# A mixture of experts after an mLSTM layer: every token through every expert, or only through its two

## The reference, cut to what matters

```python
logits = xf @ Wr + br                                   # 8 experts
topk_w, topk_idx = jax.lax.top_k(logits, 2)
topk_w = jax.nn.softmax(topk_w, axis=-1)
gate = jnp.sum(jax.nn.one_hot(topk_idx, 8) * topk_w[..., None], axis=1)
h = jax.nn.relu(jnp.einsum('th,ehf->etf', xf, W1) + b1[:, None, :])   # 128 -> 256
y = jnp.einsum('etf,efh->eth', h, W2) + b2[:, None, :]                # 256 -> 128
out = jnp.einsum('te,eth->th', gate, y)
```

## Time and profile before

| | |
|---|---|
| median of the runs | 385.41 us |
| the profiled execution | 387.64 us |
| its span, first to last instruction | 385.9 us |
| mean granted TensorE clock | 0.939 of full speed |
| bytes moved by DMA | 7.10 MB, 18 GB/s over the span |
| chain that ended last | PE 61%, DVE 23%, issue 6%, ACT 3%, POOL 3% |

### The profile page before, as it was taken

The page is one execution under the profiler, slowest core; times in us unless marked ns, Lnnn a source line. Parts: engine busy times, 40 slices in busy tenths (PEclk is TensorE's granted clock), DMA queues, the critical chain, the costliest instruction groups (busy, mean ns, idle before and its releaser), DMA issues.

```text
span 385.9 us, 6042 instructions
## 1 busy us (share of the span) xinstructions
PE 343.8 (89%) x1744; PEld 275.5 (71%) x1744; DVE 281.8 (73%) x786; ACT 227.7 (59%) x412; POOL 185.6 (48%) x180
## 2 busy tenths in 40 slices
PE   2926988999899989998999989998999899887995
PEld 2814976778687858886687868786887678665783
DVE  3787457689767986689668876897668976765664
ACT  1420232777476848586567747684857685674673
POOL 7794072148543764276326833384505641573240
PEclk9975698999899998999899989998999999998998
DMA  4840000000000000000000000000000001000000
GB/s 117 268 115 2 0 1 2 0 3 0 0 3 27 0 0 0 27 0 0 0 27 0 0 0 0 27 0 0 0 27 2 0 0 31 0 0 2 27 2 27
DMA packets 8965, 7.10 MB, mean 18 GB/s; under 512 B 1195, under 2 KB 7510, under 8 KB 8950
## 3 DMA queue, kind: packets, MB, share of 16 engines
q1 hardware_dynamic: 8722, 6.78, 6.1%
q0 software_dynamic: 64, 0.07, 0.1%
q10 hardware_dynamic: 164, 0.07, 0.1%
HBM read 4.82 MB, written 2.10 MB: 18 GB/s over the span
## 4 chain that ended last, share of the span: by engine, by line
PE 61%; DVE 23%; issue 6%; ACT 3%; POOL 3%; DMA 1%; SPq 1%; DVEq 0%; POOLq 0%
PE bank L956 7%; PE bank L958 6%; PE bank L957 6%; PE bank L984 5%; PE bank L974 5%; PE bank L975 5%; PE bank L926 5%; PE bank L994 3%; DVE hg L763 3%; PE bank L911 3%; PE bank L859 2%; PE bank L933 2%; DVE hg_lo L774 2%; DVE top_d L652 2%; DVE m_row L741 2%
## 5 line engine op out<-in xcount | busy, mean ns | idle before, releaser
L424 POOL TENSOR_TENSOR hg_lo<-hg,hg_hi 128x512 fp32r<-128x512 f32 x69 | 88.8, 1289 | 89.5 <-ACT hg_hi L494 89.5
L476 ACT ACTIVATE hid<-bank,cols 128x512 f32<-128x512 f32 x128 | 87.3, 682 | 69.4 <-PE bank L958 69.2
L763 DVE TENSOR_TENSOR hg<-hid,bank 128x512 f32<-128x512 f32 x128 | 86.7, 681 | 53.0 <-PE bank L994 32.7
L494 ACT ACTIVATE hg_hi<-hg 128x512 fp32r<-128x512 f32 x128 | 79.6, 622 | 9.0 <-DVE hg L763 8.8
L956 PE MATMUL bank<-h_hi,w_hi 128*128 (+1 forms) x128 | 58.9, 460 | 0.0
L984 PE MATMUL bank<-hg_lo,w_hi 128*128 128x512 f32 x128 | 52.6, 411 | 1.0 <-DVE hg_lo L774 0.9
L974 PE MATMUL bank<-hg_hi,w_hi 128*128 128x512 f32 x128 | 52.7, 412 | 0.0
L975 PE MATMUL bank<-hg_hi,w_lo 128*128 128x512 f32 x128 | 52.0, 407 | 0.0
L957 PE MATMUL bank<-h_hi,w_lo 128*128 (+1 forms) x128 | 51.5, 403 | 0.0
L958 PE MATMUL bank<-h_lo,w_hi 128*128 (+1 forms) x128 | 51.3, 401 | 0.0
L393 POOL TENSOR_SCALAR var_eps<-mv 128x4 f32<-128x4 f32 x16 | 4.5, 278 | 87.6 <-DVE mv L555 87.6
(11 more groups left out here) (162 smaller groups left out, 626.1 us busy)
## 6 DMA issues: line engine op xcount, KB each, us to landing
out_dram<-x_all SPq DMA_DIRECT2D x8, 256.0 KB, 2.3
w_raw<-in_L_ffn_W_dram SPq DMA_DIRECT2D x1, 1024.0 KB, 9.1
x_all<-in_L_attn_x_dram SPq DMA_DIRECT2D x2, 256.0 KB, 4.2
wmod_sb<-in_L_wmod_dram SPq DMA_DIRECT2D x1, 384.0 KB, 4.9
vo_raw<-in_L_attn_Wv_dram POOLq DMA_DIRECT2D x1, 32.0 KB, 2.8
qk_raw<-in_L_attn_Wq_dram ACTq DMA_DIRECT2D x1, 32.0 KB, 2.7
vo_raw<-in_L_attn_Wo_dram POOLq DMA_DIRECT2D x1, 32.0 KB, 3.4
qk_raw<-in_L_attn_Wk_dram ACTq DMA_DIRECT2D x1, 32.0 KB, 3.1
```

The source lines that it names most:

```text
L424: g.tensor_tensor(hg_lo[k][:, :], hg[k][:, :], hg_hi[k][:, :].bitcast(fp32), ALU.subtract).then_inc(s_lo_pool, 1)
L476: a.activation(hid[n % 4][:, :], up_bank[n % 2][:, :], ACT.Relu, bias=cols[:, R_B1 + n:R_B1 + n + 1]).then_inc(s_hid, 1)
L494: a.activation(hg_hi[k][:, :], hg[k][:, :], ACT.Copy).then_inc(s_hghi, 1)
L763: v.tensor_tensor(hg[k][:, :], hid[k][:, :], gate_bank[n // NU % 2][:, :], ALU.mult).then_inc(s_hg, 1)
```

## The change

The kernel is written anew around the routing; the mathematics of the mLSTM layer is the same. Its parts:

**Ticks.** The streams follow `TICKS` = 158 steps. Row `b` starts at tick 12·b and has steps `k` = 0 to 24; so two rows are in work at once, one in its steps 12 to 23, the next in 0 to 11.

**Slots in DRAM.** At steps 20 to 22 DVE finds the two experts of each token, PE counts with a triangular matrix how many tokens went to that expert before (L1018 to L1028), and each token has a slot number for each of its experts. At steps 23 to 30 POOL issues 8 indirect DMAs for the row (L509), each scattering 128 tokens of 512 bytes into the slots of `h_slots` of the row's group.

**Groups and blocks.** Rows (0,1), (2,3), (4,5), (6,7) are groups. When a group's rows are counted, DVE makes the list of blocks (`block_list`): 23 blocks of 128 slots, each of one expert, 92 in all. SP reads the list number by number into a register (`value_load`) and issues with it, for each block, a DMA of the 128 slots (64 KB, `xl`) and one of the expert's weights (`wl`, 128 x 642 numbers, 329 KB, from `w_all` in SBUF to SBUF), and for each group 8 DMAs of zeros behind the last token of each expert. Four blocks are a quad, two blocks a pair.

**The expert layer.** For each block PE does one transpose, two matmuls of 128 columns up and two down in plain fp32, ACT two relus of 128x128. DVE copies the transposed tokens of a quad and adds the bias to its result. SP stores a quad to `y_slots`. Pairs stand two ticks apart, and one tick apart after the last row's scatter (tick 115): group 0 has ticks 47 to 69, group 1 71 to 93, group 2 95 to 116, group 3 119 to 130.

**Gather.** For each row POOL issues 8 indirect DMAs that fetch the two results of its 512 tokens, DVE mixes them with the gate and adds them to `x`. The last two rows' gathers are at ticks 136 to 151.

Also: the scores are plain fp32 in one matmul for each block row, the maximum over time is scanned on 128 partitions (the broadcast is done by a matmul before it), the norms' scaling goes from POOL to ACT and DVE, there is no `keep_busy` and no hardware loop.

The core of the diff:

```diff
-                        t_.matmul(dst, w_hi, hx, start=True, stop=False)
-                        t_.matmul(dst, w_lo, hx, start=False, stop=False)
-                        t_.matmul(dst, w_hi, hl, start=False, stop=True).then_inc(s_up, 1)
...
-                        t_.matmul(y_bank[:, :], w_hi, hg_hi[k][:, :], start=n == 0, stop=False)
-                        t_.matmul(y_bank[:, :], w_lo, hg_hi[k][:, :], start=False, stop=False)
...
+                        for m in range(n):
+                            for u in range(NU):
+                                last = t_.matmul(u_bank[:, (m * NU + u) * P:(m * NU + u + 1) * P], wl[c % RL][:, i + m, u * P:(u + 1) * P],
+                                                 hb[c % 2][:, i + m, :], start=True, stop=True)
+                        last.then_inc(s_up, 1)
...
+            def load(c):
+                g, q0, n = QUADS[c]
+                if q0 == FIRST[g]:
+                    sp.wait_ge(s_list, g + 1)
+                    sp.wait_ge(s_spare, 16 * NG)
+                    sp.wait_ge(s_pad, 16 * E * (g + 1))
+                    for m in range(2):
+                        sp.wait_ge(s_scat[m], 16 * NSC * sum(1 for b in range(GROUPS[g][-1] + 1) if b % 2 == m))
+                if c >= RL:
+                    sp.wait_ge(s_T, c - RL + 1)
+                for i in range(n):
+                    at = sp.value_load(list_a[0:1, q0 + i:q0 + i + 1], min_val=0, max_val=SLOTS[g] - P)
+                    sp.dma_start(xl[c % RL][:, i, :], h_slots[g][bass.ds(at, P), :]).then_inc(s_xl[c % RL], 16)
+                if c >= RL:
+                    sp.wait_ge(s_y, c - RL + 1)
+                for i in range(n):
+                    e = sp.value_load(list_e[0:1, q0 + i:q0 + i + 1], min_val=0, max_val=E - 1)
+                    sp.dma_start(wl[c % RL][:, i, :], w_all[:, bass.ds(e, 1), :].rearrange("p o n -> p (o n)")).then_inc(s_wl[c % RL], 16)
...
+                        g_.indirect_dma_start(out=h_slots[GROUP_OF[b]], out_offset=bass.IndirectOffsetOnAxis(slot[:, b, i, j:j + 1], 0),
+                                              in_=h2k[b % 2][:, j, :], in_offset=None).then_inc(s_scat[b % 2], 16)
...
+                        g_.indirect_dma_start(out=yg[b % 2][:, j, i, :], out_offset=None, in_=y_slots[GROUP_OF[b]],
+                                              in_offset=bass.IndirectOffsetOnAxis(y_slot[:, b, i, j:j + 1], 0)).then_inc(s_gat[b % 2][j], 16)
```

More of the change, by code:

```diff
@@ new lines, in adaln_mlstm_moe_kernel @@
+        slot_f = sb("slot_f", [P, B, K, NT])
+        y_slot = sb("y_slot", [P, B, K, NT], u32)
+        moved = sb("moved", [P, RMAX, K, NT, E])
+        move_n = sb("move_n", [P, RMAX, K, NT])
+        blk0 = sb("blk0", [P, E])
+        shift_e = sb("shift_e", [P, E])
+        slot = sb("slot", [P, B, K, NT], u32)
+        row_n = sb("row_n", [P, E])
+        carry = sb("carry", [P, E])
+        full = [sb(f"full{g}", [P, E, MB[g]]) for g in range(NG)]
+        n_blk = sb("n_blk", [P, E])
+        end_blk = sb("end_blk", [P, E])
@@ new lines, in adaln_mlstm_moe_kernel @@
+        wl = [sb(f"wl{n}", [P, 4, NWL]) for n in range(RL)]
+        hb = [sb(f"hb{n}", [D, 4, P]) for n in range(2)]
+        hid = [sb(f"hid{n}", [P, 2, NU, P]) for n in range(2)]
+        yb = [sb(f"yb{n}", [P, 4, D]) for n in range(RY)]
+        yg = [sb(f"yg{n}", [P, NT, K, D]) for n in range(2)]
+        mix = sb("mix", [P, NT, D])
+        mix2 = sb("mix2", [P, NT, D])
+        bank = [ctx.enter_context(nc.psum_tensor(f"bank{n}", [P, 512], fp32)) for n in range(8)]
+        bA, bB, bC, bD, bE, t_bank, u_bank, y_bank = bank
@@ L188, in adaln_mlstm_moe_kernel @@
+        h_slots = [nc.dram_tensor(f"h_slots{g}", [SLOTS[g], D], fp32).ap() for g in range(NG)]
+        y_slots = [nc.dram_tensor(f"y_slots{g}", [NB[g] * P, D], fp32).ap() for g in range(NG)]
         s_small = sem("s_small")
@@ new lines, in store @@
+            def store(c):
+                g, q0, n = QUADS[c]
+                at = (q0 - FIRST[g]) * P
+                sp.wait_ge(s_y, c + 1)
+                sp.dma_start(y_slots[g][at:at + n * P, :].rearrange("(n p) d -> p n d", p=P), yb[c % RY][:, 0:n, :]).then_inc(s_ys[c % RY], 16)
+            for t in range(TICKS):
+                for g in range(NG):
+                    if t == ROW0[GROUPS[g][-1]] + 24:
+                        pads(g)
+                for c in range(len(QUADS)):
+                    if t == QUAD_T[c] - LOOK:
+                        load(c)
+                for r, (g, c, i, n, ends) in enumerate(PAIRS):
+                    if ends and t == PAIR_T[r] + 1:
+                        store(c)
+                for b in range(B):
+                    if t == GAT0[b] + NSC + S_COMB:
+                        sp.wait_ge(s_o, b + 1)
+                        sp.dma_start(out_v[:, b], x_all[:, b]).then_inc(s_out, 16)
@@ new lines, in gain_rows @@
+            def gain_rows(t):
+                if t in (6, 11):
+                    tile, n0 = ((diag_ga, 0), (diag_gb, 2))[t == 11]
+                    pe.wait_ge(s_diag, 1 + (t == 11))
+                    if t == 11:
+                        pe.wait_ge(s_gab_free, 2)
+                    for n in range(2):
+                        t_.matmul((t_bank, u_bank)[n][:, :], ones[:, :], tile[:, 4 * n:4 * n + 4, :].rearrange("p b d -> p (b d)"),
+                                  start=True, stop=True).then_inc(s_gab, 1)
@@ new lines, in _ @@
+                    if k == 23 and b == GROUPS[GROUP_OF[b]][-1]:
+                        pe.wait_ge(s_carry, b + 1)
+                        pe.wait_ge(s_pick, b + 1)
+                        t_.matmul(bE[:, 0:E], ones[:, :], carry[:, :], start=True, stop=True).then_inc(s_cnt, 1)
+                gain_rows(t)
+                for r, (g, c, i, n, ends) in enumerate(PAIRS):
+                    if t == PAIR_T[r] + 1:
+                        pe.wait_ge(s_hid, r + 1)
+                        if i == 0 and c > 0:
+                            pe.wait_ge(s_y, c)
+                        for m in range(n):
+                            for u in range(NU):
+                                at = O_W2 + u * D
+                                last = t_.matmul(y_bank[:, (i + m) * D:(i + m + 1) * D], hid[r % 2][:, m, u, :], wl[c % RL][:, i + m, at:at + D],
+                                                 start=u == 0, stop=u == NU - 1)
+                        last.then_inc(s_dn, 1)
```

1279 lines of the change are left out of this document (647 added, 632 removed).

## The result

The changed kernel takes **465.12 us** (two runs, 464.42 and 465.81) where the kernel before takes 385.41: a ratio of 1.207 with a 95% interval of 1.197 to 1.217. It is slower, outside the range of 340 to 432 us, and 90 us above the forecast of 375.

What follows compares the result with a forecast made beforehand. PE's full queue was taken as the bound, falling from 41 to 31 us a row; first pair at 102, rows to 246, last routing 289, SP's loads 337, gathers and output 376 of span: 375 us, range 340 to 432.

Steps and rivals of the forecast that it cites:

- to tick 47 (first pair): Opening and rows without experts: 29 us to tick 12, then 35/12 x 25, the first pair at 102 us.
- ticks 47 to 95, four rows: Four rows with experts: PE's 31 us each, busy at 0.86, so 36 us a row, ending at 246.
- ticks 95 to 107: Second half of the last row with group 2's experts: 30 us, ending at 276.
- last routing to group 3's first load: Eight scatters and their landing, 8 x 1.3 + 2.3, bringing the span from 276 to 289 us.
- group 3's loads: SP issues the last group's loads with nothing beside them: 46 x 1.0 + 2 = 48 us, ending at 337.
- I take 25 us: A row without expert work: 20 us for 12 ticks, lengthened to 25 because the low clock doubles the wider matmuls.
- clock above 0.9: Sign of the forecast: equal steps of rows 4 and 5 lie 36 us apart with PE's clock above 0.9.
- SP's price: Each of SP's 216 register loads with its DMA costs 1.0 us; 1.2 by the skill's floor.
- the rival of 27%: SP's register loads set the end at price x: 79 + 216x + 11, then 39 us; 431 us at 1.4; chance 27%.
- The clock rival (10%): PE runs at 1.2 GHz in the expert ticks too, a row takes 47 us, 430 in all; chance 10%.
- 31 of 36 us are busy: Argument against the clock rival: PE is busy 31 of 36 us in a row with experts.
- the packed rival: Queues pack well: rows of 32 us (-20), SP's price 0.8 (-9), POOL's DMA 0.76 (-13); two give 340 us; chance 15%.

Runs made afterwards that it cites:

- experiments 1 and 2: Changed kernel plus filler matmuls: two, four or one a tick in ticks 8 to 45, 447.45, 460.27, 454.05 us; two a tick plus fillers ahead of P x V, 448.04 us.
- second half of experiment 3: Changed kernel with one up and one down matmul per block instead of two of each: 469.73 us, ratio 1.222.
- experiment 5: Changed kernel without weight loads, 433.68 us; half of group 3's loads and its zeros on ACT, 448.99; all its loads on ACT plus two fillers a tick, 452.04.
- experiment 2: Changed kernel with two fillers a tick, plus 8 fillers ahead of step 12 and 8 ahead of step 13 (P x V) in the first three rows: 448.04 us.

## Why the prediction was wrong, step by step

The forecast had the span at 376 us; it is 462.7. The 86.7 us lie so:

| step | forecast | measured | difference |
|---|---|---|---|
| to tick 47 (first pair) | 102 | 147.4 | +45 |
| ticks 47 to 95, four rows | 144 | 164.6 | +21 |
| ticks 95 to 107 | 30 | 30.4 | 0 |
| last routing to group 3's first load | 13 | 24.1 | +11 |
| group 3's loads | 48 | 58.8 | +11 |
| from there to the end | 39 | 37.4 | -2 |

**The step that failed: "I take 25 us" for a row without expert work.** The prediction saw the mechanism: PE has only some 17 us of work in 20, and "where the opening left PE idle the clock was 0.50". It then let this double "the wider matmuls" only. The rows on which that rested were the earlier trace rows: four records of L933 in 1.20 us where eight of L859 took 1.16. They show the factor of two for a narrow matmul, and I used it for wide ones. In the changed kernel all of PE takes 1.8 to 1.9 times as long, so PE is busy 30.2 us in a row that was to take 25, stands on the chain with 28.1, and the row takes 38.2 and the next 42.3. With the clock raised by fillers, and their length taken off, the row is 24.0 to 26.6 us (experiments 1 and 2). This step was the largest, +45 us: 15 up to the first scatter (67.0 us, where the forecast's terms give 52) and 30 in the two rows behind it. I gave the clock a rival, but only for the expert ticks. Not all of the 45 us is the clock. Some 3.3 us of the longer row is the making of the first group's list, which stands on the chain on DVE (108.7 to 112.0 us) ahead of the last `ew` that P x V needs, and which the forecast had only as DVE's busy time.

**Four rows at 36 us: 38.6, 40.4, 40.0 and 45.6.** The forecast of 31 us of PE work was for the full clock; PE is busy 33 to 36 at 0.78 to 0.87, and the "clock above 0.9" did not come. The second half of experiment 3 shows that with less work the rows do not get shorter, while their clock falls. How much of the 21 us is the clock and how much is order stays open: fillers raised the clock and cost as much as they gave. PE also waits in these rows for DVE's `yb` (L861), which empties the single bank of the experts' results, 8.6 us in all up to 342 us. The longest row has the list of group 2 on its chain (270.7 to 274.0 us), with L971 at 4.53 us behind it, and six mixes of gathered results (L846); its DVE is busy 26.3 us for 18 to 21.

**The tail: SP's price was 1.0 and is 1.10 to 1.19,** and a quad's store (0.4 to 0.6) and the gaps around it come on top: 10.1 to 10.9 us a quad where the forecast's 48 us for 23 blocks make 8.3. By the floor that the Trainium skill (DMA: Bandwidth & Descriptors, Latency and other measured facts) gives a register load, some 0.6 us, the prediction made the price 1.2; its own terms, 0.6 + 0.13 + 0.38, are 1.11, an estimate. The trace agrees with the sum and not with the part: the register load itself is 0.27 us. The 11 us in front of group 3 have two parts. Row 7's eight scatters alternate on POOL with six gathers, so that the last is issued at 359.2 us, 16.7 behind the first and not 9. In the run without weight loads SP is free by then, waits 3.1 us for that scatter to land, and begins group 3 at 362.6. The rest, to 366.5, is SP's order: the 8 zero blocks at 348.4 to 357 and the last three blocks of group 2 stand ahead of the first load, and the forecast had no term for the zeros there. That SP sets the end was the rival of 27%; it decides the tail and only the tail, for without the weight loads the rows' scatters move by 1.4 us at most (experiment 5). At the measured price of 1.10 to 1.19 its own sum, 79 + 216x + 11 + 39, gives 367 to 386 us, so this rival does not explain 465 either.

**The clock rival (10%)** gave 430 us, for a clock of 0.5 in the expert ticks. It was 0.78 to 0.87 there and 0.50 to 0.52 in the 111 us before, where the rival did not look. The Trainium skill (TensorE: Matmul & The Clock Gate, What's actually happening) states that the throttled state is the default and activity releases it. The trace agrees in kind, the slices with the least expert work are the slow ones, but "31 of 36 us are busy", my argument against, is weakened by this case's own rows: PE was busy for 30.2 of 38 us at 0.50, and for 33.6 of 38.6 at 0.84.

**Right:** an indirect DMA at 1.28 us (forecast 1.3); 37.4 us from the last load on (39); the last half row of 30 us; the DMA engines never the bound, at most 0.67 of a row; and PE's prices at full clock, 0.22 to 0.27 us for a matmul of 128 columns (0.27). Two sums of the prediction do not come out: two of the three effects of the packed rival give 342 to 353 us and not 340, and 2% slower is reached at a price of 1.22 us and not 1.25.

## What to carry to other kernels

Before you cut an engine's work, ask what holds its clock up: a kernel that is one dense stream of matmuls gets the full TensorE clock, and one that computes about a third of the experts' work between waits can take longer for less. Read the clock by the length of the same matmul in two places, not by its record alone. Cost every PE term at both levels, narrow matmuls too, and sum apart the stretches in which nothing but one chain is at work. Work that is named by data costs its queue a register load and a DMA for each piece, 1.1 to 1.2 us here, and shows in the first stretch where no other work hides it; when it is moved to another engine's queue, look at what stands behind it there.

## What the runs showed of the hardware

- A nearly fully occupied PE did not keep its clock: with fillers at the head of every tick and ahead of P x V it was granted the lower level again after 23 us in which it had waited for 2 (65.6 to 88.4 us, experiment 2).
- The level falls there, and in all four rows with experts of the changed kernel, at the same place: between the products of 8 columns (L1005, at 172.2, 214.8, 251.0 and 297.8 us) and the two of 512 (L894), which then take 2.07, 1.49, 2.07 and 2.07 us for 1.12. In the four rows PE had waited 1.46 us for `h2T` and 0.28 for `lg` just before. Why it falls there is not shown. It is back 3 to 10 us later.
- The recorded clock can be wrong: 1.00 for a row whose matmuls are as long as at 0.50 (experiment 5, 72 to 110 us).
- Halving the experts' matmuls raised PE's busy time of one row from 32.5 to 34.9 us, its mean clock falling from 0.87 to 0.65; in the row before it fell from 33.6 to 31.7 us, at 0.84 and 0.74.
- Plain fp32 with 512 columns costs 0.86 us where three fp32r matmuls take 0.69 to 0.78: the split into high and low parts buys 0.6 to 1.7% of the time, and without it ACT, DVE and POOL lose 8, 7.5 and 13.8 us of work a row.
- A copy of 321 KB from SBUF to SBUF 92 times over, beside PE and the gathers, held nobody up while its issue was hidden: without it the first scatters of the rows move by 1.4 us at most (experiment 5).
